# Second attention of a gated two-layer kernel: router logits in another bank, an earlier projection on TensorE, a square root on ScalarE in place of a chain on VectorE, VectorE's rounds written out, and a last round with more banks and tiles

## The reference, cut to what matters

```python
x = x + tanh(g_xattn[0]) * xattn0(layernorm(x), ctx, pos)   # 32 heads of 8, rotary positions
x = x + tanh(g_ffn[0])   * ffn0(layernorm(x))               # shared expert and top 2 of 8 experts
x = x + tanh(g_xattn[1]) * xattn1(layernorm(x), ctx, mask)  # 16 heads of 128 over 8 key/value heads
x = x + tanh(g_ffn[1])   * ffn1(layernorm(x))               # top 2 of 8 experts, router tanh(x Wg1) Wg2
```

## Time and profile before

| what | value |
|---|---|
| median of three runs | 1771.6 us |
| the profiled execution's own time | 1754.08 us |
| its span | 1752.2 us |
| TensorE busy (matmuls) | 1546.5 us, 88% |
| VectorE busy | 1183.9 us, 68% |
| ScalarE busy | 710.0 us, 41% |
| GpSimd busy | 560.5 us, 32% |
| mean granted clock of TensorE | 0.958 |
| second attention, rounds 0 to 15 | about 873 to 1589 us of the span |

### The profile page before, as it was taken

How to read it: one execution, slowest core, us unless ns; L and a number is a source line. 1 busy time by engine, 2 the same in 40 slices (tenths; PEclk the granted TensorE clock), 3 DMA queues, 4 the chain that set the end, 5 groups by cost and what they waited for, 6 DMA issues and landing times.

```text
span 1752.2 us, 42290 instructions
## 1 busy us (share of the span) xinstructions
PE 1546.5 (88%) x14338; PEld 1310.1 (75%) x14338; DVE 1183.9 (68%) x3176; ACT 710.0 (41%) x1487; POOL 560.5 (32%) x682
## 2 busy tenths in 40 slices
PE   3899999978898899999779999989898989988987
PEld 2566666656776678899778888888788888877875
DVE  5888888886756665455467766666666666665876
ACT  2566666653222224555333333333332323344632
POOL 3555555531412230000111222222222222234556
PEclk8999999999999999999889999999999999989999
DMA  7566666661100013533300111001001001013635
GB/s 197 111 124 123 123 123 123 123 121 44 61 28 24 25 49 91 167 124 115 136 22 23 34 34 33 31 30 33 25 31 32 31 31 33 28 55 102 211 115 167
DMA packets 149017, 137.40 MB, mean 78 GB/s; under 512 B 12986, under 2 KB 138611, under 8 KB 148508
## 3 DMA queue, kind: packets, MB, share of 16 engines
q1 hardware_dynamic: 138076, 106.38, 24.6%
q0 software_dynamic: 10816, 29.54, 5.3%
HBM read 64.69 MB, written 71.19 MB: 78 GB/s over the span
## 4 chain that ended last, share of the span: by engine, by line
PE 55%; DVE 23%; issue 10%; ACT 5%; DMA 3%; SPq 2%; DVEq 1%; POOL 1%; ACTq 1%; POOLq 0%
PE bank L632 11%; PE bank L633 10%; PE bank L634 10%; PE bank L1143 4%; PE bank L694 3%; PE bank L703 2%; PE bank L1171 2%; PE bank L717 2%; PE bank L658 2%; PE bank L734 2%; DVE oT_b_lo L2548 1%; DVE probs_b L2690 1%; DVE rm_b L2687 1%; PE bank L721 1%; DVE x L2453 1%
## 5 line engine op out<-in xcount | busy, mean ns | idle before, releaser
L1848 POOL TENSOR_TENSOR probs_b<-probs_b,rs_b 128x512 f32<-128x512 f32 x64 | 66.8, 1044 | 448.1 <-DVE rs_b L2700 447.7
L1619 ACT ACTIVATE probs_b<-probs_b 128x512 f32<-128x512 f32 x64 | 40.4, 631 | 375.5 <-DVE probs_b L2690 375.5
L632 PE MATMUL bank<-xT_b_hi,m_hi 128*128 128x256 f32 x512 | 154.0, 301 | 19.2 <-ACT qT L1579 12.1
L632 PE MATMUL bank<-n_hi,oT_b_hi 128*128 128x256 f32 x512 | 155.2, 303 | 0.7 <-DVE x L2527 0.7
L633 PE MATMUL bank<-n_hi,oT_b_lo 128*128 128x256 f32 x512 | 150.8, 295 | 0.0
L634 PE MATMUL bank<-n_lo,oT_b_hi 128*128 128x256 f32 x512 | 150.3, 294 | 0.0
L633 PE MATMUL bank<-xT_b_hi,m_lo 128*128 128x256 f32 x512 | 145.8, 285 | 0.0
L634 PE MATMUL bank<-xT_b_lo,m_hi 128*128 128x256 f32 x512 | 145.7, 285 | 0.0
L1829 POOL DMA_INDIRECT xn_b<-sorted_y,place_of x62 | 60.3, 973 | 234.9 <-DMA sorted_y<-ys 182.3
L1143 PEld LDWEIGHTS bank<-ctxT_b,qT 128*128 128x128 f32 x1024 | 125.2, 193 | 2.7
L1389 ACT ACTIVATE probs_a<-probs_a 128x512 f32<-128x512 f32 x128 | 80.4, 628 | 113.8 <-DVE probs_a L2019 113.4
(11 more groups left out here) (397 smaller groups left out, 4682.1 us busy)
## 6 DMA issues: line engine op xcount, KB each, us to landing
sorted_x<-zeros SPq DMA_DIRECT2D x16, 2112.0 KB, 14.0
xg<-sorted_x SPq DMA_DIRECT2D x71, 128.0 KB, 2.1
sorted_y<-ys SPq DMA_DIRECT2D x71, 128.0 KB, 2.0
xg<-sorted_x SPq DMA_DIRECT2D x31, 256.0 KB, 3.0
sorted_y<-ys SPq DMA_DIRECT2D x31, 256.0 KB, 2.7
w_raw<-in_w SPq DMA_DIRECT2D x16, 408.0 KB, 3.8
x<-in_x SPq DMA_DIRECT2D x4, 1024.0 KB, 7.5
cx_raw<-in_ctx SPq DMA_DIRECT2D x32, 128.0 KB, 2.7
```

The costliest lines, as they stand in the source:

```text
L632: pe.matmul(dst, lh, rh, start=start, stop=False, skip_group_check=True)
L1848: pool.tensor_tensor(probs_b[b], probs_b[b], rs_b[:, b, :].unsqueeze(2).broadcast_to([P, G1, S]), ALU.mult).then_inc(s["b_probs"], 1)
```

## The change

1. TensorE, routed rounds: `project1(1,0)` goes ahead of `turn_f`, `project1(1,1)` ahead of `logits_f`, `queries1(0)` ahead of `back_f`. The logits go to bank 7.
2. VectorE: the 12 routed rounds are written out, without the loop. `add_tile` of the first tile moves from behind `otl(0)` to behind `cx_lo`, ahead of `ptl(0)`; `add_tile` of the second tile and the moments move from the round's end to ahead of `otl(2)`; `rsqrt` becomes an addition, a square root on ScalarE at the end of its round (`root_b`), a reciprocal and a product.
3. ScalarE: `cx_hi` goes ahead of `xh_f`.
4. GpSimd: both gathers of a round follow the second sequence.
5. The last round has a list of its own on three engines: transposed probabilities in banks 2, 6 and 7, outputs in banks 4 and 5 or 0 and 1, four pairs of tiles for the probabilities (in the place of `qT` and `xl_b`).
6. GpSimd, second sublayer: the eight subtractions go one by one ahead of each two indirect DMAs in blocks 5 and 6.

```diff
@@ TensorE, attend1
                 scores1(i, 1)
+                rest(project1, 1, 0)
                 if route is not None:
                     turn_f(i, route)
-                rest(project1, 1, 0)
                 scores1(i, 2)
                 ahead(turn_x1)
+                rest(project1, 1, 1)
                 if route is not None:
                     logits_f(i)
-                rest(project1, 1, 1)
+                ahead(queries1, 0)
                 if route is not None:
                     back_f(i)
-                ahead(queries1, 0)
                 scores1(i, 3)
+                if last:
+                    turn_probs1(i, 0, last)
+                    turn_probs1(i, 1, last)
+                    outputs1(i, 0, last)
+                    turn_probs1(i, 2, last)
+                    outputs1(i, 1, last)
+                    turn_probs1(i, 3, last)
+                    project1(i, 0, 0)
+                    outputs1(i, 2, last)
+                    project1(i, 0, 1)
+                    outputs1(i, 3, last)
+                    project1(i, 1, 0)
+                    project1(i, 1, 1)
+                    return
@@ ScalarE
+            def root_b(i):
+                act.wait_ge(s["stats_ready"], i + 2)
+                act.activation(sd[:, 0:4], sd[:, 0:4], ACT.Sqrt).then_inc(s["scalar_steps"], 1)
@@ ScalarE, attend1, last round
+                    w1_high(0)
+                    w1_high(1)
+                    pth(i, 0, last)
+                    pth(i, 1, last)
+                    w1_high(2)
+                    oth(i, 0, last)
...
@@ GpSimd
-                    if i + 2 < NA and b % 2 == 1:
-                        gather((i + 2) * 2 + b // 2)
+                    if i + 2 < NA and b == 1:
+                        gather((i + 2) * 2)
+                        gather((i + 2) * 2 + 1)
...
                 for t in range(FT):
+                    if i in (5, 6):
+                        down_low(i - 5, 2 * t)
@@ VectorE, attend1
                 ve.tensor_tensor(cx_lo, cx_raw, cx_hi, ALU.subtract).then_inc(s["b_cxl"], 1)
+                if more:
+                    add_tile(i * 2 + 4)
...
                 ptl(i, 0)
                 weigh(2)
                 weigh(3)
                 otl(i, 0)
-                if more:
-                    add_tile(i * 2 + 4)
...
+                if more:
+                    add_tile(i * 2 + 5)
+                    moments_b(i + 2)
+                    deviation_b(i)
                 otl(i, 2)
                 ptl(i, 3)
                 if more:
-                    add_tile(i * 2 + 5)
-                    stats_b(i + 2)
+                    shift_of_b(i)
...
-            with ve.Fori(1, NR // 2 + 1) as j:
-                st.loop(j, STEPS["b"], 1)
-                for u in range(2):
-                    attend1(j * 2 + u, route=u)
-            st.end(NR // 2 + 1)
+            for i in range(2, NR + 2):
+                attend1(i, route=i % 2)
```

More of the change, by code:

```diff
@@ L355, in build @@
         cx_hi, cx_lo, cx_raw = r.split("cx", 4, CD)
+        last_p = Region(r.at - 2 * 4 * CD - 4 * H1 * S)
+        pTh_last, pTl_last = zip(*(last_p.halves(f"pT_last{n}", 4 * P) for n in range(4)))
+        assert last_p.at <= r.at - 2 * 4 * CD
         probs_b = [r.take(f"probs_b{n}", G1, S) for n in range(4)]
@@ L366, in build, with probs_bank, probs_high, probs_low @@
         bank = [ctx.enter_context(nc.psum_tensor(f"bank{n}", [P, 512], F32)) for n in range(8)]
+        def probs_bank(b, last):
+            return bank[(2, 6, 7, 2)[b] if last else 2]
+        def probs_high(b, last):
+            return pTh_last[b] if last else pTh
+        def probs_low(b, last):
+            return pTl_last[b] if last else pTl
+        def out1_bank(b, par, last):
+            return bank[par if last and b % 2 else 4 + par]
         def turned(i):
@@ L1148, in turn_probs1 @@
                 pe.wait_ge(s["b_probs"], START + i * NB + b + 1)
-                pe.wait_ge(s["b_pTh"], START + i * NB + b)
-                pe.wait_ge(s["b_pTl"], START + i * NB + b)
+                if not last or b in (0, 3):
+                    before = 1 if last and b == 3 else b
+                    pe.wait_ge(s["b_pTh"], START + i * NB + before)
+                    pe.wait_ge(s["b_pTl"], START + i * NB + before)
                 if b == 0:
@@ L1581, in q_copy, with pth, oth @@
                     s["b_q_ready"], 1)
[L1583 removed]
+            def pth(i, b, last=False):
                 act.wait_ge(s["b_pT_psum"], START + i * NB + b + 1)
[L1585 to L1588 removed]
+                act.wait_ge(s["b_o_psum"], START + i * NB * 2 + (0 if last else 2 * b))
+                if last:
+                    act.wait_ge(s["b_scores"], START + NA * NB)
+                act.activation(probs_high(b, last), probs_bank(b, last)[:, :], ACT.Copy).then_inc(s["b_pTh"], 1)
+            def oth(i, b, last=False):
                 if b % 2 == 0:
@@ L1621, in next_q @@
                 def next_q(*cs):
[L1622 to L1627, removed]
+                    for c in cs:
+                        q_copy(i + 1, c)
                 expo(0)
@@ L1640, in attend1 @@
                 act.activation(cx_hi, cx_raw, ACT.Copy).then_inc(s["b_cxh"], 1)
+                if route is not None:
+                    xh_f(i)
                 expo(2)
@@ L1646, in attend1 @@
                 expo(3)
+                if last:
+                    w1_high(0)
[4 more added lines that the diff above has]
+                    oth(i, 0, last)
+                    pth(i, 2, last)
+                    w1_high(3)
+                    oth(i, 1, last)
+                    pth(i, 3, last)
+                    w1_high(4)
+                    w1_high(5)
+                    oth(i, 2, last)
+                    w1_high(6)
+                    w1_high(7)
+                    oth(i, 3, last)
+                    return
                 next_q(0)
@@ L1658, in attend1 @@
                 next_q(7)
+                if not late and not last:
+                    root_b(i)
             xT_high1(0)
@@ L2729, in attend1 @@
                 ve.tensor_tensor(cx_lo, cx_raw, cx_hi, ALU.subtract).then_inc(s["b_cxl"], 1)
+                if more:
+                    add_tile(i * 2 + 4)
+                if last:
+                    weigh(2)
+                    ptl(i, 0, last)
+                    weigh(3)
+                    ptl(i, 1, last)
+                    otl(i, 0, last)
+                    resid1(i - 1, 1)
+                    ptl(i, 2, last)
+                    otl(i, 1, last)
+                    ptl(i, 3, last)
+                    otl(i, 2, last)
+                    moments1(i - 1)
+                    otl(i, 3, last)
+                    return
                 ptl(i, 0)
```

64 lines of the change are left out of this document (33 added, 31 removed).

## The result

| | kernel before | changed kernel |
|---|---|---|
| median of four runs each, same chip | 1771.53 us (1767.56 to 1773.22) | 1714.48 us (1711.23 to 1719.13) |
| the profiled execution's own time | 1754.08 us | 1711.23 us |
| its span | 1752.2 us | 1709.4 us |
| TensorE busy | 1546.5 us, 88% | 1532.6 us, 90% |
| ScalarE busy | 710.0 us, 41% | 750.4 us, 44% |

The ratio is 0.9679, 95% interval [0.9661, 0.9696]: 57.1 us less, where 63.4 were forecast. The profile of the kernel before is not one of these four runs: its execution was 17 us shorter than their median. The time lies 6.3 us above the forecast of 1708.2 and inside the forecast's own range.

The account below looks back on a forecast made before the run. The prediction took TensorE, busy 88% of the span, as the bound, with its waits in routed rounds also costing clock. Its terms summed to -63.4 us, from 1771.6 to 1708.2 us; own range 1697 to 1719, 8 in 10 1692 to 1733.

Parts of the forecast that it names:

- The wait before turn_f: Routed rounds: TensorE's whole wait for the router's normalised rows goes, by shorter chain, loop removal and 24 matmuls ahead: -34.3 us.
- rival C: Routed rounds written out: VectorE stalls on fetching its own new code, two stalls a round cost 74 us, 1782 us; chance 0.05.
- The wait before outputs1(1): Routed rounds: without the first add_tile ahead of it, ptl(1) is 1.03 us earlier and TensorE's 0.7 us wait goes: -8.4 us.
- queries1(2): Routed rounds: TensorE's wait for q_copy(0) grows, as centre(3) starts 0.45 us late, 12 times: +5.4 us, bounds 0 and +12.
- The clock: Routed rounds: without the long waits the granted clock stays high, 11 times 1.55 us: -17.1 us, bounds 0 and -17.1.
- Rival A: Routed rounds: the longer wait before queries1(2) keeps the clock low, the 17.1 us are not returned, 1725 us; chance 0.18.
- The square root: ScalarE, 14 rounds: two function table loads and a small activation a round fit in idle time: cost 0, bound +10 us.
- The gathers: GpSimd, routed rounds: the second gather waits for the first add_tile but lands in time: cost 0, bound +6 us.
- rival B: Routed rounds: ScalarE's root, reload and loop edge, or the gathers' landing, are late, 10 + 6 us, 1724 us; chance 0.11.
- The last round: Last round: waits as long as before but fewer short ones, so low clock ends sooner: -3.7 us, bounds +1 and -8.
- The second sublayer: Second sublayer: with GpSimd's subtractions spread, one of each four holds VectorE's chain: -5.3 us, bounds 0 and -8.

Follow-up runs that it names:

- the pair of repetitions: The kernel before and the changed kernel, both unchanged, run again for second profiles: 1750.37 us and 1692.43 us, ratios 0.9999 and 0.9678 to the kernel before.

## Why the prediction was right, and where it was off

1. *The wait before turn_f* (-34.3): right, all of it went. The reasons were shared out wrongly. The loop's removal alone took 20 us of the waits, where five edges of 3.08 us make 15.4, and `project1(1,0)` first took the rest. The shorter chain, the first of the three that I named, was not needed: with it back on VectorE nothing changes. With the loop gone either of the other two does nearly all: 0.2 us a round is left with VectorE's shorter round end alone, nothing with the projection alone. What the Trainium skill says of loops bears on this (Runtime: NRT & Kernel Launch, "Instruction fetch mechanics": a taken branch breaks the sequential prefetch, code in line is streamed). The runs agree: 3.08 us at a pass's edge, none in the rounds written out. It also speaks against rival C. That the 3.08 us are a fetch the profile does not name, but a transfer of instructions falls into each of the five idle times (DMA view, 1136.87 to 1139.95 us and 1229.18 to 1232.23). It fits without proving it, as other such transfers fall where VectorE is busy:
```profile
q14 instruction: 1, 0.01, 0.9%
...
q14 instruction: 1, 0.01, 1.1%
```
2. *The wait before outputs1(1)* (-8.4): right. Written out alone, VectorE's rounds bring 3.3 of it; that the early `add_tile` brings the rest was not isolated.
3. *queries1(2)* (+5.4): +4.8 in sum, 0.79 to 1.18 us each. The reason is shown: the old place of the router's products gives 0.32 of it back each time. The static addresses saved nothing here; the wait is 0.86 with them.
4. *The clock* (-17.1): from the first `turn_f` to the last, eleven rounds, the pair of repetitions is 52.2 us apart (504.57 and 452.39). Waits make 36.3 of it (33.0 + 7.7 - 4.4). The rest, 15.9 us, is the clock in the main: ten of the eleven intervals before hold a low stretch, at some 1.5 us each. Rival A did not come: the waits before query products, eleven of 1.18 us and one of 1.35, left the clock at 1.00. One reading behind this term was wrong. Of the waits before `turn_f` in the earlier trace rows it was the one of 1.67 us, not that of 1.56, that the full clock followed; all six of 1.55 or 1.56 us in that profile were followed by the low level. The length of the wait alone does not decide: in the run without the loop three of twelve waits of 1.21 us were followed by it, and 1.35 here and 1.67 there were not. What does, no run shows.
5. *The square root*: 0, right, with 3.03 us of ScalarE's idle time left. Each load took 1.28 us with nothing behind it, and TensorE waited for nothing of it.
6. *The gathers*: 0, right; no wait for one stands in TensorE's list, and `add_tile` hid nothing else; rival B is refuted in both halves.
7. *The last round* (-3.7): from the last `turn_f` on, the stage is 5.0 us shorter in the repetitions (120.4 and 115.4), part of it the routed round's own end. The three waits were 3.7, 1.0 and 2.5 (1.5 for the second in the repetition) for the 3.8, 1.2 and 2.3 forecast.
8. *The second sublayer* (-5.3): this is the step that failed. "I let one subtraction of each four hold it" was wrong for one of the two blocks in most profiles: where TensorE waits 6.7 us, three of four met the chain, at 1.9, 1.7 and 1.3 us, 4.9 in all, where the row of four had cost 5.92 - 0.68 = 5.2 in one operation. Where it waits 3.7 us, one did. The old price was too high as well: in the other profiles with the old place the operation of 5.92 us cost TensorE 2.31 us, not 3.91. The price was in the main moved, not divided; what it brought is about 1 us, less than the 4.7 us by which profiles with the new place differ.

The attention of the repetitions is 56.6 us shorter; with 1 us for term 8 that makes 57.6, and the medians are 57.1 and 57.9 us apart. Of the 6 us by which the forecast was too low, 4 are term 8 and 1 the clock; the rest is within what medians tell.

## What to carry to other kernels

Write out a hardware loop on an engine whose round feeds the bounding one, before anything in the round is moved; here that was over half of the gain. Count a wait with the clock that it costs, and from several cases: waits of 1.18 us cost only themselves here, those of 1.21 us another 1.5 us in three of twelve cases, those of 1.56 us in nearly all, and single ones of 1.35 and 1.67 us only themselves. When a block of work that locks another engine out is split, put each piece where the other engine has slack: between links of its chain a piece of 1.3 us cost 1.3 to 1.9 us, and with the pieces in slack the stage was 3 us shorter, which the whole time could not confirm.

## What the runs showed of the hardware that was not expected

- With its loop gone VectorE also lost small idle times: in the short rounds of the kernel before, the normalised rows and the next row maxima start 0.31 and 0.22 us late, in the version without the loop they mostly follow at once (VectorE's timelines, first before, then without the loop). That this, and so addresses from registers, is what took the waits from 1.56 to 1.21 us is likely but was not isolated.
```profile
1189.99 0.73 DVE L2462 TENSOR_SCALAR g_xn<-x,rr_b,shift_b 128x256 f32 x2 [0.31 <-DVE xn_b L2462]
1190.94 0.69 DVE L2687 TENSOR_REDUCE rm_b<-bank 128x8 f32<-128x512 f32 x1 [0.22 <-DVE g_xn L2462]
```
```profile
1171.17 0.74 DVE L2462 TENSOR_SCALAR g_xn<-x,rr_b,shift_b 128x256 f32<-128x256 f32 x2
1172.05 0.69 DVE L2687 TENSOR_REDUCE rm_b<-bank 128x8 f32<-128x512 f32 x1
```
- A VectorE operation on 128x4 values can be held for a whole GpSimd subtraction: 2.03 and 1.85 us in place of 0.17 and 0.16, above. The statistics beside the first subtraction of the block were not (1.41 us for four, beside a subtraction or without one).
- The same kernel takes 1752 us in two groups of runs and 1771 us in two others. The five profiles of the second kind have the stall near 453 us, two idle times of VectorE of 2.0 us without a releaser between 655 and 662 us, and others of about 2 us in the last sublayer. Blocks of the second sublayer that take 31.8 us in the first kind take 32.6 or 33.4 in them, and 33.4 in the first profile of the kernel before. What makes all this is open.
